# A scan kernel on one core: the three matmuls of a softplus sum set on steps of their own, and the sum over the state taken once for two steps

## The reference

```python
delta = softplus(dt_w @ dts + dt_b)           # per direction, channel, token
h = h * exp(delta * A) + (delta * u) * B      # over the 64 tokens of the window
y = sum over n of h * C                       # then + D * u
y = y0 + y1 + y2 + y3                         # directions put back in place
out = x + alpha * (h_in + (LN(y) * silu(z)) @ out_proj)
```

## Time and profile before

| | |
|---|---|
| median of three executions | 31193.54 us |
| profiled execution, its time | 31207.2 us |
| its span | 31205.5 us |
| TensorE (PE) busy | 29499.7 us, 95% |
| VectorE (DVE) busy | 27691.9 us, 89% |
| GpSimd (POOL) busy | 25850.6 us, 83% |
| ScalarE (ACT) busy | 23949.0 us, 77% |
| mean granted TensorE clock, share of full speed | 0.993 |
| DMA | 3048.53 MB, mean 98 GB/s |

### The profile page before, as it was taken

The page is one execution under the profiler, slowest core; times in us unless marked ns, Lnnn a source line. Parts: engine busy times, 40 slices in busy tenths (PEclk is TensorE's granted clock), DMA queues, the critical chain, the costliest instruction groups (busy, mean ns, idle before and its releaser), DMA issues.

```text
span 31205.5 us, 1063977 instructions
## 1 busy us (share of the span) xinstructions
PE 29499.7 (95%) x437486; PEld 11409.7 (37%) x437486; DVE 27691.9 (89%) x18447; ACT 23949.0 (77%) x37630; POOL 25850.6 (83%) x13288
## 2 busy tenths in 40 slices
PE   8999899999999999999999999999999999999999
PEld 2333333333333333333333333333333333333333
DVE  7888799989989899989999999999998989999998
ACT  4555688778878878778878787878887878887887
POOL 0000599999999999999999999999999999999999
PEclk9999999999999999999999999999999999999999
DMA  3333344444444444444444444444444444444444
GB/s 82 88 88 79 79 100 99 100 99 100 100 100 100 99 100 100 101 98 101 99 101 99 102 98 101 100 102 98 103 98 101 99 101 99 103 98 102 98 102 90
DMA packets 3822186, 3048.53 MB, mean 98 GB/s; under 512 B 2184849, under 2 KB 2987793, under 8 KB 3796945
## 3 DMA queue, kind: packets, MB, share of 16 engines
q1 hardware_dynamic: 3809888, 2910.77, 44.2%
q0 software_dynamic: 8560, 77.41, 0.7%
HBM read 2325.71 MB, written 449.58 MB: 89 GB/s over the span
## 4 chain that ended last, share of the span: by engine, by line
PE 28%; POOL 26%; issue 18%; DVE 7%; ACT 6%; DMA 3%; SPq 1%; POOLq 0%; ACTq 0%; DVEq 0%
POOL state L942 21%; PE dbu L1032 10%; PE pp L1129 6%; PE yb L1054 5%; DVE state L1478 5%; POOL dd L949 3%; ACT state L1259 3%; DMA cc<-cd 2%; DVE dg L1468 2%; PE pp L1103 2%; PE pp L1092 1%; POOL dd L962 1%; POOL yf L978 1%; PE pp L1123 1%; ACT ye L1284 1%
## 5 line engine op out<-in xcount | busy, mean ns | idle before, releaser
L942 POOL TENSOR_TENSOR state<-state,cc 128x1024 f32<-128x1024 f32 x9408 | 22044.9, 2373 | 1586.5 <-DVE state L1478 1366.0
L1478 DVE TENSOR_TENSOR_SCAN state<-state,dbu 128x1024 f32<-128x1024 f32 x9408 | 21060.6, 2271 | 2266.4 <-PE dbu L1032 2022.2
L1259 ACT ACTIVATE state<-dl,a_neg 128x512 f32<-128x512 f32 x18816 | 12253.9, 711 | 26.1 <-DMA dl<-dlx 1.2
L1032 PE MATMUL dbu<-dg,du_t 64*32 64x256 f32 x301056 | 10377.9, 383 | 758.7 <-DVE state L1478 661.9
L1032 PEld LDWEIGHTS dbu<-dg,du_t 64*32 64x32 f32 x301056 | 4765.7, 106 | 7121.7 <-issue 6026.0
L1054 PE MATMUL yb<-state,mask 128*32 128x256 f32 x75264 | 6026.8, 392 | 34.5 <-ACT ye L1358 29.9
L1468 DVE TENSOR_TENSOR dg<-b_t,mask_q 128x1024 f32<-128x1024 f32 x3136 | 3759.0, 1199 | 41.2 <-PE b_t L1071 41.2
L1054 PEld LDWEIGHTS yb<-state,mask 128*32 128x32 f32 x75264 | 1484.6, 108 | 3916.5 <-issue 3488.6
L229 POOL DMA_DIRECT2D act_d<-acted x32 | 16.2, 507 | 3214.4 <-DVE mixed L489 2906.3
L1129 PE MATMUL pp<-sp_a,minus 128*128 128x512 f32 x2352 | 1322.2, 644 | 509.3 <-ACT ye L1284 197.8
L1340 ACT ACTIVATE sp_y<-pp 128x512 f32<-128x512 f32 x1176 | 699.1, 594 | 1404.7 <-PE pp L1129 1404.7
(11 more groups left out here) (171 smaller groups left out, 26576.2 us busy)
## 6 DMA issues: line engine op xcount, KB each, us to landing
dl<-dlx SPq DMA_DIRECT2D x4704, 256.0 KB, 4.6
cc<-cd SPq DMA_DIRECT2D x3136, 256.0 KB, 6.3
dlx<-dd SPq DMA_DIRECT2D x1176, 256.0 KB, 2.0
shifted<-in_x SPq DMA_DIRECT2D x384, 392.0 KB, 12.5
xs<-ye SPq DMA_DIRECT2D x1176, 112.0 KB, 2.9
xs<-ye SPq DMA_DIRECT2D x588, 128.0 KB, 2.9
image<-in_x SPq DMA_DIRECT2D x32, 1176.0 KB, 24.5
act_d<-acted POOLq DMA_DIRECT2D x32, 1176.0 KB, 9.1
```

What stands on the lines that cost most here:

```text
L942: nc.gpsimd.tensor_tensor(its, its, cc[:, h, s, :], ALU.mult).then_inc(hc_done, 1)
L1032: last = nc.tensor.matmul(dst[:, :, TQ * e:TQ * e + TQ], du_t[its, j, col:col + JC], dg[its, h, 2 * k + s, MG * TQ * g:MG * TQ * g + MG * ...
L1259: nc.scalar.activation(state[:, slot, :, m * WPX:m * WPX + WPX].rearrange("p (q k) t -> p q k t", k=2), by_place(dl[:, J // 2, 2 * h + J % ...
L1478: nc.vector.tensor_tensor_scan(its, its, dbu[p % 2][:], 0.0, ALU.mult, ALU.add).then_inc(scan_done, 1)
```

## The change

`sum_states` runs on every second step of TensorE's loop, when both halves of a unit are there: four matmuls of 512 columns for the unit in place of two times four of 256. `ysum_done` counts units, and the four waits on it are rewritten to that count. The three matmuls of a softplus sum get a step each from `SUM_AT`, counted from the chain's first step; some chains have two or three of them on one step. `small_part` follows on the step of the last. The second `x_in` moves from step 16 to 17.

```diff
-S_XIN, S_CONV, S_SILU, S_XD, S_Z = [11, 16], [21, 24], 27, [32, 44], [42, 45]
+S_XIN, S_CONV, S_SILU, S_XD, S_Z = [11, 17], [21, 24], 27, [32, 44], [42, 45]
-L_LOG, L_SUM, L_U = 1, 3, 5
+L_LOG, L_U = 1, 5
+SUM_AT = {(1, 0): (3, 4, 5), (1, 1): (2, 3, 4), (1, 2): (3, 3, 4), (0, 0): (2, 3, 4), (0, 1): (3, 3, 3), (0, 2): (3, 3, 3)}
...
+        def sums_at(b, p, i):
+            due = []
+            for first, f, j in CHAINS:
+                at = first + SUM_AT[f, j][i]
+                T = b + 1 - f - at // STEPS1
+                if at % STEPS1 == p and has(T):
+                    due.append((T, f, j))
+            return due
...
                 def sum_states(T, p):
-                    f, J, h, slot, s = unit(p)
+                    f, J, h, slot, _ = unit(p)
                     bank = yb[J % 2]
                     pe.wait_ge(hc_done, T * STEPS1 + p + 1)
-                    if s == 0 and h == 0 and (later(T) or 6 * f + J > 1):
+                    if h == 0 and (later(T) or 6 * f + J > 1):
                         pe.wait_ge(ye_done, T * (2 * NJC) + 6 * f + J - 1)
-                    at = 128 * (1 - s if h else s)
                     for m in range(MG):
-                        src = state[:, slot, WPS * s:WPS * s + WPS, m * WPX:m * WPX + WPX].rearrange(
-                            "p (v k) t -> p k v t", k=2)
-                        dst = halves(bank[JC * m:JC * m + JC, :])[:, :, at:at + 128].rearrange("p k (v t) -> p k v t", t=WPX)
-                        last = nc.tensor.matmul(dst, mask[:], src[:, ::-1, ::-1, ::-1] if h else src,
-                                                start=h == 0 and s == 0, stop=h == 1 and s == 1)
-                    if f == 0 and h == 0 and s == 1:
+                        src = state[:, slot, :, m * WPX:m * WPX + WPX].rearrange("p (q k) t -> p k q t", k=2)
+                        last = nc.tensor.matmul(bank[JC * m:JC * m + JC, :].rearrange("p (k q t) -> p k q t", k=2, t=WPX),
+                                                mask[:], src[:, ::-1, ::-1, ::-1] if h else src, start=h == 0, stop=h == 1)
+                    if f == 0 and h == 0:
...
-                def exponent(b, T, f, j):
-                    free_bank(b, f"m{f}{j}")
-                    pe.wait_ge(sp_act, chain(T, f, j) + 1)
-                    for i, part in enumerate((sp_a, sp_w, sp_v)):
-                        last = nc.tensor.matmul(pp[:], minus[:, i, :], part[:], start=i == 0, stop=i == 2)
-                    last.then_inc(pp_ready, 1)
+                def exponent(b, T, f, j, i):
+                    if i == 0:
+                        free_bank(b, f"m{f}{j}")
+                        pe.wait_ge(sp_act, chain(T, f, j) + 1)
+                    part = nc.tensor.matmul(pp[:], minus[:, i, :], (sp_a, sp_w, sp_v)[i][:], start=i == 0, stop=i == 2)
+                    if i == 2:
+                        part.then_inc(pp_ready, 1)
...
-                    for T, f, j in chains_at(b, p, L_SUM):
-                        exponent(b, T, f, j)
+                    for i in range(3):
+                        for T, f, j in sums_at(b, p, i):
+                            exponent(b, T, f, j, i)
...
-                        if has(done):
+                        if has(done) and (p - LAG) % 2:
                             sum_states(done, (p - LAG) % STEPS1)
...
-                        act.wait_ge(ysum_done, (T * UNITS + U - NSLOT) * 2 + 2)
+                        act.wait_ge(ysum_done, T * UNITS + U - NSLOT + 1)
...
-                        for T, f, j in chains_at(b, p, L_SUM):
+                        for T, f, j in sums_at(b, p, 2):
                             small_part(b, T, f, j)
```

More of the change, by code:

```diff
@@ L1291, in conv_silu @@
                         act.wait_ge(hd_done, chain(b, 1, NJ - 1) + 1)
-                        act.wait_ge(ysum_done, (b * UNITS + PHASE_J.index(NJC - 1)) * 2 + 2)
+                        act.wait_ge(ysum_done, b * UNITS + PHASE_J.index(NJC - 1) + 1)
                     nc.scalar.activation(u[:], pre, ACT.Silu).then_inc(u_done, 1)
@@ L1350, in y_bank @@
                 def y_bank(T, f, J):
-                    act.wait_ge(ysum_done, T * STEPS1 + SPP * f + 2 * (UPP - PHASE_J[::-1].index(J)))
+                    act.wait_ge(ysum_done, T * UNITS + UPP * f + UPP - PHASE_J[::-1].index(J))
                     if f == 1 and J == 0 and has(T + 1):
```

## The result

The changed kernel takes 32082.06 us (median of 4 executions, 32070.77 to 32107.94) against 31188.98 of the kernel before on the same chip: ratio 1.0287, interval 1.0269 to 1.0305. Forecast were 31,685 with a range up to 32,080, which the time passes by 2. The direction and the place of the first loss were right; the loss of 893 us was nearly twice the 490 forecast.

The account below looks back on a forecast made before the run. PE was taken to give the pace on average, no engine far ahead. The hold on step 35 was to cost 2.5 us a tile, times 196 tiles 490 us on the profiled 31207, so 31,685; range 31,060 to 32,080.

Parts of the forecast that it names:

- The wait on step 35: PE stands 2.25 us for ScalarE's second logarithm before chain (0, 0)'s sum; 2.5 us a tile lost.
- each by its price above: Work queued behind step 35's wait keeps its earlier durations: about 1.0 us each for `inputs`, unit and sum matmul.
- The hold of (1, 1): On step 14 PE stands 1.4 us for the logarithms; hidden by later waits, else 0.6 to 1.4 a tile.
- So it costs nothing: Step 14's wait is covered by PE's 1.45 us wait for DVE on step 28 and ScalarE's string.
- rival C: Slower by more: step 14's wait isn't hidden, 3.9 us a tile, 31,960, to 32,200 with dear units; 19%.
- The sign given for C: PE's wait on step 28 has gone and the tile takes 144 us or more.
- The units: Eight sum-over-state instructions of 512 columns take 1.00 us against 1.14, saving 3.4 us a tile.
- the saving lies mostly where PE waits again: Argument against no change: the saved PE work falls mostly where PE then waits; that work falls 2.0 us a tile.
- Apart costs 0.4 for three matmuls: Three softplus sum matmuls on separate steps take 3.18 us against 2.77 together; some 1.4 us a tile more.
- the burst on step 8: Chain (1, 0)'s sum spread from step 8: scan 10 goes 1.7 us earlier, scan 12 unchanged; no gain, no loss.
- Rivals A and B: First: PE's work decides, 2.0 us a tile saved, 30,800, 17%. Second: the hold cancels that, 31,190, 9%.

Follow-up runs that it names:

- e5: The changed kernel with the softplus sums of chains (0, 0) and (1, 1) whole on steps 36 and 15, second `x_in` still on 17: ratio 0.9960.
- e1: The changed kernel with the three matmuls of chain (0, 0)'s softplus sum together on step 36, as before the change: ratio 1.0055.
- e4: The changed kernel with two more matmuls, whose results nobody reads, ahead of the wait on step 35: ratio 1.0194.
- e2: The changed kernel with every softplus sum whole on its chain's third step and `x_in` back on step 16, leaving only the sum over the state per unit: ratio 0.9958.
- e7: The kernel before with the whole softplus sum of chain (0, 0) on step 35 instead of 36: ratio 1.0188.
- e9: The changed kernel with ScalarE's two affine passes over y on steps 34 and 35 instead of 33 and 34: ratio 1.0179.
- e8: As e2 (only the sum over the state per unit), but with chain (1, 0)'s softplus sum on steps 8, 9 and 10: ratio 0.9990.
- e3: The changed kernel with `sum_states` and the `ysum_done` waits as before the change, leaving the spread softplus sums and later second `x_in`: ratio 1.0363.
- e6: The changed kernel with `b_columns` ahead of the softplus sum in the same step, on steps 35 and 10: ratio 1.0174.
- e10: As e7, with two more matmuls whose results nobody reads, placed in PE's wait on step 35: ratio 1.0142.

## Why the prediction was right in direction and too low

The ledger, in us a tile, by the ratios, each to the kernel before on its own chip (in brackets by the mean tiles, which mix chips): units and the two spread sums -0.6 (-0.8) (e5); the sum of (1, 1) early and apart, e1 less e5, +1.5 (+1.7); the sum of (0, 0) early and apart, without the clock, e4 less e1, +2.2 (+2.3); the clock, changed less e4, +1.5 (+1.2). Together +4.6 (+4.5). Each is good to some 0.3.

The traces show where in a tile it goes. Each figure is the median over the tiles in which the clock doesn't fall, in us; the first part runs from the fifth scan behind `center` to the 31st, the second from there to the fifth of the next tile:

| kernel | first part | second part |
|---|---|---|
| before | 77.4 | 63.1 |
| e2, units only | 77.0 | 63.2 |
| e5, no sum early | 76.9 | 63.2 |
| e1, (1, 1) early | 78.5 | 63.2 |
| changed, both early | 78.5 | 65.4 |
| e7, (0, 0) early, alone | 77.6 | 65.4 |
| e4, filler | 78.8 | 65.4 |

The 0.4 us that e4's first part has over the changed kernel's stand ahead of the filler, and no run explains them. Over all tiles the second part alone has a mean of 67.45 us in the changed kernel and 65.91 in e4, which puts the clock at 1.5 again.

- **The wait on step 35**, forecast at 2.25 us with `b_columns` and `inputs` behind it: right, 2.12 with both behind it. Its price was put at 2.7 late at step 5 of the next tile, 2.5 in the sum; the second part grows by 2.3. That ScalarE's string sets it: right, e9.
- **The clock**: the first step that failed. The prediction prices every matmul behind the hold at its duration from rows at a granted clock of 1.00, "each by its price above", and among the rivals is none in which an idle PE comes back slower. It costs 1.2 to 1.5 us a tile, some 240 to 290 us of the 893. The rows of before could have raised it: the longest idle time of PE that they show is 1.45 us, and the change puts over 2 us on one place of every tile.
- **The hold of (1, 1)**: the second step that failed. The prediction found the wait (1.4 us; it is 1.05) and said "So it costs nothing", since PE waits for DVE on step 28 anyway. But the hold makes DVE late, and a wait of PE for DVE can't cover that (the rows under e5). The first part was to end where it did before; it is 1.0 us longer than before and 1.6 longer than in e5. This is the mechanism of rival C, on top of a forecast that otherwise held; so without the clock the time is between the forecast and C's 31,960 (e4: 31,843), and with it above both. The sign given for C, that the wait on step 28 has gone, was only half there: it is 1.05 us for 1.45.
- **Luck**: that the range's end, 32,080, comes within 2 us of the time is luck. It was as wide as it was for rival C; no term stood for the clock.
- **The units**: 1.00 forecast for the eight instructions, 0.99 measured. That "the saving lies mostly where PE waits again" was right: 3.4 us less work gave 0.5 to 0.7 (e2). The falls of the clock that the units bring were not foreseen.
- **Apart costs 0.4 for three matmuls, and the burst on step 8 isn't what the tile loses by**: e8 agrees, 0.1 to 0.5 us more for one chain.
- **Rivals A and B**: fell; PE's work is less and the time is more.

What stays open: why the same wait of 2.12 us lets the clock fall in some tiles and not in others; and why e3 loses 0.8% or 1.2 to 1.4 us a tile more than the changed kernel. More falls of the clock (104 against 89) are the smaller part of it: in tiles without one e3 takes 145.0 us where the changed kernel takes 143.8, with 0.8 of the difference in the first part. So the units save more beside the holds than they do alone (e2); no run shows by which wait.

## What to carry to other kernels

A wait on an engine that works in order costs what is queued behind it, and where the engine is TensorE it may cost again once it is over, since matmuls behind an idle stretch can run at half speed: price a new wait with both. Before a matmul is moved earlier, read the time from its operand's end to its start in the trace (0.6 us here) against the step it is moved by (over 2). And when slack is to hide a cost, ask whose lateness it covers: an engine's wait for another can't make up for what makes the other late.

## What the runs showed of the hardware that I had not expected

Behind one and the same idle time of 2.12 us the granted TensorE clock was 1.00 in one tile and 0.50 to 0.54 for some 7 us in another; `inputs` then took 1.96 us for 1.09, a unit 1.93 for 1.06. Four matmul instructions without a use, 1.56 us, ahead of the wait kept it at 1.00 and made the whole kernel 0.9% faster.

How often the clock fell within or just behind one idle time of PE, in 195 tiles each (194 where the idle time is below 1 us):

| idle time, us | kernel | tiles with a fall there |
|---|---|---|
| 2.12 | changed | 106 |
| 1.98 | e3 | 123 |
| 1.98 | e7 | 61 |
| 1.72 (step 28) | e2 | 42 |
| 1.41 | e9 | 19 |
| 1.11 | e6 | 31 |
| 0.63 | e4 | 0 |
| 0.49 | e10 | 0 |

The length of the idle time alone doesn't settle it: 1.98 us gave 123 and 61, and 1.11 more than 1.41.
